# Experts' gated rows scattered and added into a table, and a last norm that loads the sums

## What is computed

```python
    def _L0_ffn_ref(x, gate_w, gate_b, w1, b1, w2, b2, gamma, beta):
        gate_logits = x @ gate_w + gate_b
        topk_vals, topk_idx = jax.lax.top_k(gate_logits, K)
        topk_w = jax.nn.softmax(topk_vals, axis=-1)
        h = jax.nn.relu(jnp.einsum('bsh,ehf->bsef', x, w1) + b1)
        expert_out = jnp.einsum('bsef,efh->bseh', h, w2) + b2
        sel = jnp.take_along_axis(expert_out, topk_idx[:, :, :, None], axis=2)
        moe = jnp.sum(topk_w[..., None] * sel, axis=2)
        y = x + moe
        ...
        return (y - mu) / jnp.sqrt(var + EPS) * gamma + beta
    ...
    x = x + _L0_ffn_ref(_layernorm(x, axis=-1)[None], ...)[0]
```

## Time and profile before

| | us |
|---|---|
| median of 3 runs | 1938.82 (1937.65 to 1941.0) |
| the profiled execution | 1941.34 |
| its span, first to last instruction | 1939.4 |
| busy in the span: PE, DVE, ACT, POOL | 1445.2, 969.4, 463.1, 994.3 |
| mean granted TensorE clock | 0.858 |

### The profile page before, as it was taken

One profiled execution on the slowest core, in us unless ns is written; L12 is line 12 of the kernel. 1 busy time (PEld: TensorE's weight loads), 2 busy tenths in 40 slices (PEclk: granted clock), 3 DMA queues, 4 the chain that ended last, 5 costly groups with the idle time before them and its releaser, 6 DMA issues. The chain is left out here.

```text
span 1939.4 us, 33213 instructions
## 1 busy us (share of the span) xinstructions
PE 1445.2 (75%) x7648; PEld 1164.5 (60%) x7649; DVE 969.4 (50%) x3112; ACT 463.1 (24%) x1295; POOL 994.3 (51%) x1125
## 2 busy tenths in 40 slices
PE   5499968787769887877878788664899999996000
PEld 4366636565657665665756666442799899886000
DVE  8766556552737452742745275368211222221787
ACT  0144432121112111211212112010344444443000
POOL 0200027777777777777777777720233233223775
PEclk9799987989788899888899879775899999998555
DMA  6000043333333333333333333344322333532443
GB/s 215 1 0 0 0 144 104 104 106 103 103 105 104 103 103 105 103 104 105 103 103 105 105 101 105 104 132 137 113 78 70 113 94 95 189 92 64 131 137 115
DMA packets 105690, 193.84 MB, mean 100 GB/s; under 512 B 19056, under 2 KB 68976, under 8 KB 105520
## 3 DMA queue, kind: packets, MB, share of 16 engines
q0 software_dynamic: 47520, 129.82, 23.9%
q1 hardware_dynamic: 58128, 63.58, 9.8%
HBM read 159.11 MB, written 34.21 MB: 100 GB/s over the span
## 5 line engine op out<-in xcount | busy, mean ns | idle before, releaser
L701 POOL DMA_INDIRECT ring<-table,staged x784 | 747.5, 953 | 242.8 <-issue 226.3
L976 PE MATMUL bank<-ring,hots 128*128 x1372 | 323.9, 391 | 53.0 <-SPq L690 52.7
L976 PEld LDWEIGHTS bank<-ring,hots 128*128 128x128 f32 x1372 | 264.6, 195 | 102.7 <-issue 66.9
L1427 PEld LDWEIGHTS bank<-xT,w 128*128 128x128 f32 x1696 | 208.9, 194 | 15.5 <-issue 10.3
L1427 PE MATMUL bank<-xT,w 128*128 128x128 f32 x1696 | 210.2, 278 | 8.7 <-issue 8.7
L976 PE MATMUL bank<-ring,late_hots 128*128 x388 | 141.8, 518 | 97.4 <-SPq L690 88.8
L1405 ACT ACTIVATE hT<-bank,b 128x128 f32<-128x128 f32 x424 | 155.6, 367 | 226.0 <-PE bank L1427 202.4
L1435 PE MATMUL bank<-w,hT 128*128 128x256 f32 x848 | 201.7, 381 | 1.5 <-DVE y L1468 1.4
L786 DVE TENSOR_SCALAR hots<-iota_t,edge_l 128x128 f32<-128x128 f32 x686 | 182.1, 362 | 1.8
L976 PEld LDWEIGHTS bank<-ring,late_hots 128*128 128x128 f32 x388 | 92.5, 252 | 138.9 <-issue 124.3
L1348 POOL COPY at_x<-list 128x1 int32 (+1 forms) x108 | 19.6, 181 | 287.4 <-DVE xin L1450 201.2
(11 more groups left out here) (256 smaller groups left out, 2028.9 us busy)
## 6 DMA issues: line engine op xcount, KB each, us to landing
w<-in_w SPq DMA_DIRECT2D x32, 512.0 KB, 5.2
lists_out<-y SPq DMA_DIRECT2D x106, 128.0 KB, 2.7
ring<-table,staged POOLq DMA_INDIRECT x784
x<-in_x SPq DMA_DIRECT2D x1, 6272.0 KB, 23.4
table<-xn SPq DMA_DIRECT2D x7, 896.0 KB, 4.4
rows<-xn SPq DMA_DIRECT2D x1, 6272.0 KB, 21.1
out<-out_c SPq DMA_DIRECT2D x7, 512.0 KB, 3.1
out<-out_c SPq DMA_DIRECT2D x7, 384.0 KB, 2.6
```

The lines of the kernel that those rows point to most:

```text
L701: pool.indirect_dma_start(out=ring[:, j, :], out_offset=None, in_=a.table, in_offset=bass.IndirectOffsetOnAxis(ap=staged[:, half, col:col ...
L976: last = nc.tensor.matmul(agg, hot[:, k, :], two[:, k, :], start=False, stop=False)
L1427: last = nc.tensor.matmul(up_ps[fc], w1[:, slot, ch, fc * P:(fc + 1) * P], xT[:, ch, :], start=(ch == 0), stop=(ch == DC - 1))
```

## The change

**Gates travel with the rows.** The table `rows` gets two more columns, the row's two gates, written by a second transfer on SP (D to D+2) once the gates are there. A gathered row is now 258 values. The list holds 2 x row + (0 or 1) + 1 while it is built; `route` splits that into `m.list[..., 0]` (row to fetch), `m.which` (which gate it is), and `m.list[..., 1]` (row to add to, shifted by LAG = 3 blocks; places without a row point to 128 spare rows at the end of `sums`). This takes the steps on `spot`, `first_i`, `unused` and `which`, of which the diff shows the first and the last.

**Sums in place of lists.** `lists_out` and its blanks are gone. A DRAM table `sums` is preset with `m.xn` by SP, behind the weights of the first four experts. For each block DVE picks the gate in `rows_in` (two steps on 2 and 1 values a row), writes the product with bias to `biased`, and multiplies it by the gate into one of two buffers `y`. POOL, not SP, sends `y` off by an indirect transfer that adds it to the rows of `sums`. Each of these waits until the one before has landed. With an even number of blocks one dummy block follows, whose rows all point to the spare rows.

**The last norm** is no block of code of its own: its programs for SP, ACT and DVE stand behind the experts' own. SP loads finished sums four tiles at a time, up to 16 tiles ahead. DVE takes statistics of one group and then finishes the group before. The reciprocal root comes from ACT's Ln and Exp, from one table set loaded ahead. The memory of the graph part is given back before the experts, which makes room for its buffers.

```diff
 BLOCKS = 2 * NP // BLOCK + E
-AHEAD = 2
+LAG = 3
...
         @block.sync
         def _(sp):
-            sp.dma_start(a.rows.rearrange("(t p) d -> p t d", p=P), m.xn[:]).then_inc(rows_out, 16)
+            rows = a.rows.rearrange("(t p) d -> p t d", p=P)
+            sp.dma_start(rows[:, :, 0:D], m.xn[:]).then_inc(rows_out, 16)
+            sp.wait_ge(gates_ok, 1)
+            sp.dma_start(rows[:, :, D:D + 2], m.share[:]).then_inc(rows_out, 16)
             sp.dma_start(e.b1[:], a.b1).then_inc(e.b1_in, 16)
             for slot in range(e.slots):
                 e.load(sp, slot, slot)
-            sp.wait_ge(rows_out, 16)
+            sp.wait_ge(zeros_ok, 2)
+            sp.dma_start(a.sums[NP:NP + P], e.zero_row[:]).then_inc(e.sums_in, 16)
+            sp.dma_start(a.sums[0:NP].rearrange("(t p) d -> p t d", p=P), m.xn[:]).then_inc(e.sums_in, 16)
+            sp.wait_ge(rows_out, 32)
...
-            c.add(dve.tensor_tensor(m.share[:, :, 1], eg[:], m.share[:, :, 0], ALU.mult))
+            dve.tensor_tensor(m.share[:, :, 1], eg[:], m.share[:, :, 0], ALU.mult).then_inc(gates_ok, 1)
...
-                    dve.tensor_scalar(ids[part][:, :, 0], hi_hot[part][:], m.const[:, C_LANE:C_LANE + 1], None, ALU.mult)
+                    dve.tensor_tensor(ids[part][:, :, 0], hi_hot[part][:],
+                                      lane2[:, None, None, :].broadcast_to([P, n, BLOCKS, 2]), ALU.mult)
...
-            c.add(dve.tensor_scalar(tokens[:], list_ps[:, BLOCKS:2 * BLOCKS], float(P), None, ALU.mult))
-            c.wait()
-            c.add(dve.tensor_tensor(m.list[:, 0:BLOCKS], tokens[:], list_ps[:, 0:BLOCKS], ALU.add))
+            c.add(dve.tensor_scalar(tokens[:], list_ps[:, BLOCKS:2 * BLOCKS], float(2 * P), None, ALU.mult))
+            c.wait()
+            c.add(dve.tensor_tensor(tokens[:], tokens[:], list_ps[:, 0:BLOCKS], ALU.add))
+            c.wait()
+            c.add(dve.tensor_copy(spot[:], tokens[:]))
...
+            c.add(dve.tensor_copy(m.list[:, 0:BLOCKS, 0], spot[:]))
+            c.add(dve.tensor_tensor(m.list[:, LAG:LAG + BLOCKS, 1], spot[:], unused[:], ALU.add))
             c.wait()
...
         @block.gpsimd
         def _(pool):
             pool.sem_inc(copied, 2)
-            pairs = nc.s_assert_within((of_list(pool, 1, E - 1) + 3) // 2, (E + 3) // 2, (BLOCKS + AHEAD) // 2,
-                                       skip_runtime_bounds_check_because="half of all blocks and two more")
-
-            def fetched(u):
+            pool.sem_inc(y_free, 3)
+            pairs = nc.s_assert_within(of_list(pool, 1, E - 1) // 2, E // 2, BLOCKS // 2,
+                                       skip_runtime_bounds_check_because="half of all blocks")
+
+            def fetched(b, n):
+                pool.wait_ge(copied, b + 1)
+                settle(pool, m)
+                pool.tensor_copy(at[:, n, :], m.list[:, bass.ds(b, 1), :].rearrange("p a k -> p (a k)")).then_inc(at_ok, 1)
+                pool.wait_ge(at_ok, b + 1)
+                settle(pool, m)
+                pool.indirect_dma_start(out=got[:, n, :], out_offset=None, in_=a.rows,
+                                        in_offset=bass.IndirectOffsetOnAxis(ap=at[:, n, 0:1], axis=0)).then_inc(x_in[n], 16)
+
+            def landed(times, n):
+                pool.wait_ge(x_in[n], times * 16)
...
+            def sent(of, n):
+                pool.wait_ge(y_ok, of + 2)
+                if not isinstance(of, int) or of > 0:
+                    pool.wait_ge(y_out, of * 16)
+                    pool.sem_inc(y_free, 1)
+                settle(pool, m)
+                pool.indirect_dma_start(out=a.sums, in_=y[:, 1 - n, :], in_offset=None, compute_op=ALU.add,
+                                        out_offset=bass.IndirectOffsetOnAxis(ap=at[:, n, 1:2], axis=0)).then_inc(y_out, 16)
+
...
+            pool.wait_ge(e.sums_in, 32)
+            sent(0, 1)
+            with pool.Fori(0, pairs) as i:
                 for n in range(2):
-                    b = u * 2 + n
...
+                    fetched(i * 2 + (n + 4), n)
+                    landed(i + (n + 2), 1 - n)
+                    sent(i * 2 + (n + 1), n)
+            pool.wait_ge(y_out, pairs * 32 + 16)
+            pool.sem_inc(sums_ok, 1)
+            pool.wait_ge(x_in[1], pairs * 16 + 32)
+            settle(pool, m)
...
         @block.sync
         def _(sp):
-            def sent(i, more):
-                bounds = bounds_of(sp, i)
+            with sp.Fori(0, E // SLOTS - 1) as i:
                 for slot in range(SLOTS):
-                    first, end = bounds[slot:slot + 2]
-                    with sp.Fori(first, end) as b:
-                        sp.wait_ge(y_ok, b + 2)
-                        sp.dma_start(rows_of(a.lists_out, b), y[:]).then_inc(y_out, 16)
-                        sp.sem_inc(filled, 16)
-                    if more:
-                        e.load(sp, i * SLOTS + (slot + SLOTS), slot)
-
-            sp.sem_inc(y_out, 16)
-            end = of_list(sp, 1, E - 1)
-            sp.wait_ge(blank_ok, 1)
-            with sp.Fori(end, BLOCKS) as b:
-                sp.dma_start(rows_of(a.lists_out, b), blank[:]).then_inc(filled, 16)
-            with sp.Fori(0, E // SLOTS - 1) as i:
-                sent(i, True)
-            sent(E // SLOTS - 1, False)
-            end = of_list(sp, 1, E - 1)
-            sp.wait_ge(y_out, end * 16 + 16)
-            settle(sp, m)
-            sp.wait_ge(filled, BLOCKS * 16)
+                    end = of_list(sp, 1, i * SLOTS + slot)
+                    sp.wait_ge(y_ok, end + 1)
+                    settle(sp, m)
...
+                    e.load(sp, i * SLOTS + (slot + SLOTS), slot)
+            sp.wait_ge(sums_ok, 1)
+            last_norm.sync(sp)
 
...
-                        pe.wait_ge(y_ok, b + 1)
+                        pe.wait_ge(biased_ok, b + 1)
...
 
-                dve.tensor_tensor(tile(m.x1, t), tile(m.x1, t), m.vecs[:, V_FBETA:V_FBETA + D], ALU.add)
-
-            dve.memset(blank[:], 0.0).then_inc(blank_ok, 1)
+                dve.scalar_tensor_tensor(tile(m.x1, t), tile(m.x1, t), 1.0, m.vecs[:, V_FBETA:V_FBETA + D], ALU.mult, ALU.add)
+
...
                 dve.wait_ge(got_ok, b + 1)
                 if not isinstance(b, int) or b > 0:
                     dve.wait_ge(xtr_ok, b)
                     settle(dve, m)
-                dve.tensor_copy(xin[:], got[:, bass.ds(b % 2, 1), :].rearrange("p a d -> p (a d)")).then_inc(copied, 1)
-
+                dve.tensor_tensor(pick[:, bass.ds(b % 2, 1), :], got[:, bass.ds(b % 2, 1), D:D + 2], m.which[:, bass.ds(b, 1), :],
+                                  ALU.mult).then_inc(pick_ok, 1)
+                dve.tensor_copy(xin[:], got[:, bass.ds(b % 2, 1), 0:D].rearrange("p a d -> p (a d)"))
+                dve.wait_ge(pick_ok, b + 1)
+                settle(dve, m)
+                dve.tensor_tensor(gate[:, bass.ds(b % 4, 1)], pick[:, bass.ds(b % 2, 1), 0:1].rearrange("p a k -> p (a k)"),
+                                  pick[:, bass.ds(b % 2, 1), 1:2].rearrange("p a k -> p (a k)"), ALU.add).then_inc(copied, 1)
+
+            dve.sem_inc(biased_ok, 1)
             dve.sem_inc(y_ok, 1)
...
                         rows_in(b + 2)
                         dve.wait_ge(down_ok, b + 1)
-                        dve.wait_ge(y_out, b * 16 + 16)
-                        dve.tensor_tensor(y[:], down_ps, b2[:, slot, :], ALU.add).then_inc(y_ok, 1)
+                        dve.tensor_tensor(biased[:], down_ps, b2[:, slot, :], ALU.add).then_inc(biased_ok, 1)
+                        dve.wait_ge(biased_ok, b + 2)
+                        dve.wait_ge(y_free, b + 2)
+                        settle(dve, m)
+                        dve.tensor_scalar(y[:, bass.ds(b % 2, 1), :].rearrange("p a d -> p (a d)"), biased[:], gate[:, bass.ds(b % 4, 1)],
+                                          None, ALU.mult).then_inc(y_ok, 1)
+            dve.wait_ge(y_free, of_list(dve, 1, E - 1) + 2)
+            settle(dve, m)
+            dve.sem_inc(y_ok, 1)
+            last_norm.vector(dve)
+
+
...
-                    for j in range(j0, j1):
-                        pool.wait_ge(z_ok, g * 7 + (j + 1))
-                        settle(pool, m)
-                        for k in range(2):
-                            pool.indirect_dma_start(out=got[:, j, k, :], out_offset=None, in_=a.lists_out,
-                                                    in_offset=bass.IndirectOffsetOnAxis(ap=at[:, j, k:k + 1], axis=0)
-                                                    ).then_inc(back[part], 16)
...
+    def sync(self, sp):
+        sums = self.a.sums[0:NP].rearrange("(t p) d -> p t d", p=P)
+        out_v = self.a.out.rearrange("(t p) d -> p t d", p=P)
+        ahead = self.LOADED // 4
...
+        for q in range(ahead):
+            load(q)
+        for q, (t0, t1) in enumerate(self.batches):
+            if q + ahead < len(self.batches):
+                load(q + ahead)
+            sp.wait_ge(self.out_ok, q + 1)
```

(35 more changed lines are left out.)

249 lines of the change are left out of this document (109 added, 140 removed).

## The result

| | before | after |
|---|---|---|
| median, us | 1938.24 (1936.24 to 1941.0) | 2091.97 (2090.87 to 2092.24, 4 runs) |
| profiled execution, span, us | 1939.4 | 2089.0 |
| mean granted TensorE clock | 0.858 | 0.859 |

The changed kernel takes 1.0791 times as long (95% interval 1.0772 to 1.081): 154 us slower. The forecast was 2042 us, slower, with a range of 1975 to 2150. Direction and mechanism held, and the time lies in the range, 50 us above the point.

The account below looks back on a forecast made before the run. TensorE bounds the experts' loop before the change, and a ring of waits through POOL and DVE after it. 1941.3 + 164 (loop) - 69 (last norm) + 8 (routing) = 2044, less 2.5 to the median: 2042 us, range 1975 to 2150.

Parts of the forecast that it names:

- The ring: Experts' loop: y, scatter, gather, release, rows_in and the next y wait on one another, 5.4 us a block; chance 0.7.
- The loop: Experts' loop: 105 turns of 5.4 us in place of 402.9 us, +164 us (+91 to +269).
- y's end to the scatter's start: Experts' loop, handover from DVE's y to POOL's scatter: between 0.54 and 0.79 us, taken 0.65.
- scatter's start to the gather's start: Experts' loop, POOL: scatter priced like a gather at 0.97 us, then index copy and gap; 2.04 us.
- gather's start to DVE's pick: Experts' loop: POOL's gather, 0.97 us, then 0.2 us from its end to DVE; 1.17 us.
- biased and the wait on it: Experts' loop, DVE: biased 0.43 us and a wait on it 0.15 us with registers to work out; 0.58 us.
- my signs of being wrong: Experts' loop: blocks under 4.4 us apart, or a scatter taking POOL much more or less than 0.97 us.
- The landing as a rival: Experts' loop: the scatter's landing sets the turn, from a landing of 4.75 us; at 5.5 us, 2121 us; chance 0.2.
- The ring doesn't close: Experts' loop: POOL's and DVE's steps are short enough, TensorE stays the bound at 3.84 us, 1878 us; chance 0.05.
- TensorE's clock: Experts' loop: the clock falls to 1.2 GHz in the gaps, a block takes 7.5 us, 2263 us; chance 0.05.
- The last norm: Stage behind the experts' loop: 98 gathers and two passes a tile gone, 159.7 us to 91, -69 us (60 to 75 gained).
- Routing: Stage ahead of the experts: small DVE list steps +4 us, gates and presetting of sums in the open 4 us; +8 us.

Follow-up runs that it names:

- plain_scatter: The changed kernel with POOL's scatter overwriting instead of adding, so no sums are made: 5.39 us a turn against 5.94, 2342.03 us on a slower chip.
- lag4_plain: The changed kernel with POOL scattering block b-4 instead of b-3, and overwriting instead of adding (no sums): 3.87 us a turn, 1872.84 us.
- lag4: The changed kernel with POOL scattering block b-4 instead of b-3: 5.00 us a turn against 5.94, ratio 1.0265 to the kernel before on the same chip.

## Where the prediction held and where it didn't

**Direction and cause: right, and shown.** The ring was read from the order of the instructions and the waits, and the waits of after are those that were forecast. Opening it in either of two places gives a microsecond a block back; a step on it costs, and the same step on the open ring costs nothing.

**The loop, +164 forecast, +220.5 measured: the term that was mis-sized.** Between two undisturbed y:

| step | forecast | measured |
|---|---|---|
| y's end to the scatter's start | 0.65 | 0.98 |
| scatter's start to the gather's start | 2.04 | 2.59 |
| gather's start to DVE's pick | 1.17 | 0.41 |
| pick to biased | 0.55 | 0.59 |
| biased and the wait on it | 0.58 | 0.91 |
| y | 0.45 | 0.35 |
| sum | 5.44 | 5.83 |

- The scatter was priced like a gather, 0.97 us; it takes POOL 1.59. From its start to the gather's start that makes 2.59 us against 2.04, and plain_scatter, with 2.00, shows that the adding is all of it. The upper end that I gave, 1.3, was too low as well: no row showed an adding transfer, and I had no reason to stop there. A scatter much above 0.97 us was one of my signs of being wrong. It came, and it was wrong about the price, not about the ring.
- The gather's own 0.97 us is not on the ring. Pick starts 0.41 us after the gather, while POOL shows it busy for 1.01. I read DVE's start at 1366.05, 0.05 us after a gather's end, as the order of the two. It isn't in the loop. At the start of the experts POOL's release more likely waited for the first gather's landing, 3.0 us after its start at 1363.07, and the two ends met by chance: in after the same pick starts at 1367.29, 2.9 us after the first gather's start and ahead of the second gather's end at 1367.36. This error of 0.76 us hid others of the opposite sign, and that was luck. With that step right and the rest priced as it was, the turn would have been 4.68 us and the forecast 1966 us, below my own range.
- The handovers were too short: from y to POOL's scatter by 0.33, and on DVE from biased to y, where it is idle for 0.48 us and I had 0.15 and another 0.1 in the step of y. I took both gaps from rows of another kind. That the registers worked out behind the wait make the difference is likely, and no run shows it apart.

With the small differences of the table they make 105 x 0.39 = 41 us. 4 us more are the rounding from 5.44 to 5.4. The remaining 12 us are turns above 5.83 (105 x (5.94 - 5.83)): one of 7.34, some dozen between 6.0 and 6.8, mostly near the loads of weights, and some twenty at 5.94 to 5.97.

**The landing as a rival (0.2): not the case, but close behind.** I had 4.75 us from start to start. Two scatters in a row at the end of after give it (timeline):

```profile
2003.00 1.59 POOL L1402 DMA_INDIRECT sums<-y,at_x  x1 [2.25 <-DVEq L1530]
...
2007.54 1.59 POOL L1402 DMA_INDIRECT sums<-y,at_x  x1 [0.94 <-DMA sums<-y,at_x]
2011.28 9.57 SPq L1570 DMA_DIRECT2D zin<-sums  x5
2014.94 1.41 DVE L1600 BATCH_NORM_STATS2 st_c<-zin 128x6 f32<-128x256 f32 x4 [12.92 <-DMA zin<-sums]
```

4.54 us: by the updates of its semaphore the first lands 3.66 us after its start, and 0.88 us later the second starts. Over all of after the median to landing is 3.84 us, and a gather's is 2.8. So the microsecond that I added for the target was right, 4.1 us a little long and 0.65 to start again a little short. The Trainium skill (DMA: Bandwidth & Descriptors, Anatomy of one DMA) led to an estimate of 2.3 us; the median of 3.84 us is 1.5 us above it, and only the plain scatter of lag4_plain, 2.43 us, comes near. The Trainium skill's page Collectives: The Full Stack (Why ReduceScatter is half of AllGather) gives the two source reads of an add as the reason for half the rate; that points the right way, since lag4 needs 4.6 us and more from start to start and lag4_plain at most 3.4 in its quiet turns.

**"The ring doesn't close", 1878 us (0.05): not the case.** But the figure is what an open ring gives once the landing is short too, 1872.84 us in lag4_plain. The ends of the ring were added up wrongly: the lower ends of the steps as they stand make 5.0 us, not 4.7, and the upper ends 6.3, not 6.4. So the lower end of the range should have been some 30 us higher, and for a turn of 4.42 us the scatter would have had to cost POOL under 0.4 us, not 0.7.

**TensorE's clock (0.05): not the case.** It was granted 0.93 in the loop with PE busy 78%, near the 0.91 of the earlier trace rows. This costs nothing here, since PE waits.

**The last norm, -69 forecast, -72.8 measured.** A group takes 5.81 us (5.9 put), and statistics begin 12.9 us after the last y (14 put).

**Routing, +8 forecast, +1.9 measured.** The list's steps ended 1.3 us later (1362.3 against 1361.0), since short steps of DVE start 0.12 to 0.25 us apart and not 0.27. The gates and the preset kept the DMA engines busy all through the stage (share 1.11, where it was 0.51), but ended in time; the 4 us that I had in the open were none. The gates, 6272 pieces of 8 bytes, landed 21.9 us after their issue, and rows, beside them, took 28.1 us where it had taken 21.1.

## What to carry to other kernels

When a change hands a result to an engine whose queue also feeds the producer, write down the cycle of waits before adding up busy times: POOL was busy 295 of 623 us here, TensorE had the same matmuls, and the loop took 55% longer. Then find what else is late: the order, the landing and POOL's own row lay at 5.8, 4.7 and 3.9 us, so mending the first alone leaves a kernel that is still slower than before. Take handovers of a price from rows in which the waiting instruction stands in the same kind of loop, and give an operation that no row shows an upper end well beyond its nearest relative.
